# Turning attention probabilities with VectorE's block transposes and SBUF-to-SBUF transfers in a two-layer transformer kernel

## The reference, cut to what matters

```python
def _L0_ffn_ref(x, q_w, k_w, v_w, o_w, sel_v_w, sel_o_w, route_scale):
    H, E, P, K = (8, 8, 128, 2)
    gate_v = _get_sel_gate(x, sel_v_w, rs)      # [b, s, h, e], two of eight experts not zero
    gate_o = _get_sel_gate(x, sel_o_w, rs)
    xv = jnp.einsum('bsd,hedp->bshep', x, v_w.reshape(H, E, D, P))
    v = jnp.einsum('bshep,bshe->bhsp', xv, gate_v)
    att = jax.nn.softmax(jnp.einsum('bhqp,bhkp->bhqk', q, k) * SCALE, axis=-1)
    ctx = jnp.einsum('bhqk,bhkp->bqhp', att, v)
    weighted = ctx[:, :, :, None, :] * gate_o[..., None]
    out = jnp.einsum('bshep,hepd->bsd', weighted, o_w.reshape(H, E, P, D))
```

## Time and profile before

| | us |
|---|---|
| median of 3 runs | 3138.77 |
| lowest, highest run | 3130.59, 3141.73 |
| span of the profiled execution | 3102.4 |
| PE busy in it | 2958.3 |
| DVE busy | 2183.4 |
| ACT busy | 1926.7 |
| POOL busy | 1838.9 |

### The profile page before, as it was taken

One profiled execution on the slowest core, in us unless ns is written; L12 is line 12 of the kernel. 1 busy time (PEld: TensorE's weight loads), 2 busy tenths in 40 slices (PEclk: granted clock), 3 DMA queues, 4 the chain that ended last, 5 costly groups with the idle time before them and its releaser, 6 DMA issues. The chain is left out here.

```text
span 3102.4 us, 53399 instructions
## 1 busy us (share of the span) xinstructions
PE 2958.3 (95%) x17672; PEld 2071.1 (67%) x17672; DVE 2183.4 (70%) x4152; ACT 1926.7 (62%) x4366; POOL 1838.9 (59%) x2333
## 2 busy tenths in 40 slices
PE   4999999999999999999999999999999987899998
PEld 2666666666666666666666666666667675567675
DVE  7777888877778888777788887777777655235243
ACT  1576666676667666666666666666666743353634
POOL 2466666676666666676766676666666645433330
PEclk7899999999999999999999999999999989899999
DMA  5000001100100011001000110011001011233222
GB/s 171 21 22 23 22 22 33 32 23 26 44 26 22 23 32 33 23 23 37 29 22 22 33 32 23 23 37 29 23 22 40 16 42 44 65 96 104 86 77 87
DMA packets 140048, 124.71 MB, mean 40 GB/s; under 512 B 28662, under 2 KB 122304, under 8 KB 139680
## 3 DMA queue, kind: packets, MB, share of 16 engines
q1 hardware_dynamic: 127312, 88.75, 10.2%
q0 software_dynamic: 10160, 30.17, 3.1%
q10 hardware_dynamic: 2304, 2.36, 0.4%
HBM read 97.47 MB, written 29.28 MB: 41 GB/s over the span
## 5 line engine op out<-in xcount | busy, mean ns | idle before, releaser
L1340 DVE TENSOR_REDUCE m_peaks<-m_ring 128x1 f32<-128x512 f32 x1024 | 636.7, 681 | 95.3 <-PE m_ring L299 95.1
L1072 ACT ACTIVATE m_expA<-m_ring 128x512 f32<-128x512 f32 x1024 | 536.3, 607 | 120.5 <-PE m_ring L372 102.3
L933 POOL TENSOR_TENSOR m_vprod<-m_vprod 128x512 f32<-128x512 f32 x256 | 334.3, 1306 | 451.5 <-DVE m_vprod L1353 327.1
L1043 ACT ACTIVATE m_prob<-m_ring,m_negs 128x512 f32<-128x512 f32 x512 | 350.8, 691 | 285.9 <-DVE m_negs L1388 285.4
L943 POOL TENSOR_TENSOR m_oprod<-m_oprod 128x512 f32<-128x512 f32 x256 | 329.4, 1287 | 258.9 <-ACT m_oprod L1012 255.2
L350 PE MATMUL m_ring<-m_probT,m_vs 128*128 128x256 f32 x2048 | 464.4, 380 | 5.8 <-DVE m_vprod L1353 5.2
L350 PEld LDWEIGHTS m_ring<-m_probT,m_vs 128*128 128x128 f32 x2048 | 386.3, 190 | 68.4 <-issue 13.3
L1378 DVE TENSOR_REDUCE m_negs<-m_ring 128x1 f32<-128x512 f32 x512 | 344.3, 684 | 115.3 <-PE m_ring L105 113.2
L1353 DVE TENSOR_TENSOR m_vprod<-m_ring,m_gate 128x512 f32<-128x512 f32 x512 | 342.2, 687 | 112.4 <-PE m_ring L105 99.5
L1053 ACT ACTIVATE m_probT<-m_ring 128x512 f32<-128x512 f32 x512 | 294.0, 610 | 63.2 <-PE m_ring L338 61.8
L1012 ACT ACTIVATE m_oprod<-m_ring,m_go 128x128 f32<-128x128 f32 x1024 | 292.0, 372 | 34.6 <-PE m_ring L105 23.7
(11 more groups left out here) (322 smaller groups left out, 5558.3 us busy)
## 6 DMA issues: line engine op xcount, KB each, us to landing
m_wraw<-in_v_w SPq DMA_DIRECT2D x32, 512.0 KB, 4.1
m_qf<-q_dram SPq DMA_DIRECT2D x128, 128.0 KB, 2.7
m_wraw<-in_o_w SPq DMA_DIRECT2D x32, 512.0 KB, 4.3
q_dram<-m_kf SPq DMA_DIRECT2D x24, 256.0 KB, 4.4
listed<-in_pad SPq DMA_DIRECT2D x6, 897.0 KB, 11.5
m_xg<-listed SPq DMA_DIRECT2D x39, 138.0 KB
m_rows<-answers SPq DMA_DIRECT2D x8, 512.0 KB, 4.1
sums_dram<-m_sumsT ACTq DMA_DIRECT2D x128, 18.0 KB
```

The source lines that it names most:

```text
L933: vchain(pool.tensor_tensor(vprod[:, 0:512], vprod[:, 0:512], vprod[:, 512:1024], ALU.add))
L1043: act.activation(prob[t % 2][:, c * 512:(c + 1) * 512], ring.home["scores", n, t, c][:, :], ACT.Exp, bias=neg[t % 2], accum_out=den[n % 2] ...
L1072: act.activation(expA[hh][:, c * 512:(c + 1) * 512], ring.home["scT", n, k, hh, c][:, :], ACT.Exp)\
L1340: v.tensor_reduce(peaks[:, t, hh, c:c + 1], ring.home["peaks", n, t, hh, c][:, :], AX.X, ALU.max)\
```

## The change

- `turn` and `keep_turned` are gone. DVE turns a whole tile of probabilities with one instruction, `turn_probs` (128x1024). It transposes each block of 32x32 on its own and writes to a single tile `turned`, which holds a group of two query tiles.
- SP carries the blocks to their places in `move_probs`: 16 transfers a group, one for each pair of 32-row blocks (a, b), each 32 partitions by 8 pieces of 64 elements (256 B). `probT` is one tile instead of two. A move waits for both transposes of its group and for the `weigh` before it; `weigh` waits for the move; `turn_probs` of an even tile waits for the move of the group before.
- The queries of a group now lie in `probT` in blocks of 32 that alternate between the two tiles. `keep_ctx` and `lower_ctx` put them back through their access patterns.
- `gate_outputs` on DVE is left for tiles 1, 3, 5 and 7. For even tiles ACT scales both halves.
- The order on every engine is new, and so is the place of the loads on SP. `load_layer1` comes one head earlier.

The new functions, from the diff:

```diff
+                def turn_probs(n, t):
+                    if n not in steps:
+                        return
+                    k = TPB * n + t
+                    v.wait_ge(probs_made, 2 * k + 2)
+                    if t % 2 == 0 and k:
+                        v.wait_ge(probs_moved[(k // 2 - 1) % 2], moved(0, k // 2 - 1))
+                    v.transpose(turned[:, :, t % 2, :], prob[t % 2][:, :].rearrange("p (c r) -> p c r", r=32))\
+                        .then_inc(probs_turned, 1)
...
+                def move_probs(n, g):
+                    if n not in steps:
+                        return
+                    sp.wait_ge(probs_turned, 8 * n + 2 * g + 2)
+                    if 4 * n + g >= 1:
+                        sp.wait_ge(ctx_made, 4 * n + g)
+                    by_key = turned[:, :, :, :].rearrange("p (k b) t j -> p b k (t j)", b=4)
+                    for a in range(4):
+                        for b in range(4):
+                            sp.dma_start(probT[32 * b:32 * b + 32, :, 64 * a:64 * a + 64],
+                                         by_key[32 * a:32 * a + 32, b, :, :]).then_inc(probs_moved[g % 2], 16)
...
-                    pe.wait_ge(probT_kept, 16 * n + 4 * g + 4)
+                    pe.wait_ge(probs_moved[g % 2], moved(n, g))
...
-                def scale_outputs(n, t):
+                def scale_outputs(n, t, c):
...
-                for i in steps:
-                    load_queries(i + 1)
-                    load_outputs(i)
-                    if i + 2 in steps:
-                        load_values(i + 2)
+                for i in range(-5, N0 + 5):
+                    load_values(i + 1)
+                    move_probs(i - 1, 3)
+                    load_queries(i + 1)
+                    move_probs(i, 0)
+                    if i == N0:
+                        load_early_heads()
+                    if i == N0:
+                        load_early_rden()
+                    batch_loads(i)
+                    move_probs(i, 1)
+                    load_outputs(i)
+                    move_probs(i, 2)
```

More of the change, by code:

```diff
@@ L225, in layer0 @@
         den = [m.sbuf(f"den{k}", [P, TPB, 2]) for k in range(2)]
-        probT = [m.sbuf(f"probT{k}", [P, TPB, 2 * P]) for k in range(2)]
+        probT, turned = m.sbuf("probT", [P, TPB, 2 * P]), m.sbuf("turned", [P, T // 32, 2, 32])
         ctxT = [m.sbuf(f"ctxT{k}", [PS, 2, 2 * P]) for k in range(2)]
@@ L1773, in _ @@
+                    find_largest(i + 2, 3, 0)
+                    gate_values(i + 3, 2, 0)
+                    find_largest(i + 2, 3, 1)
+                    gate_values(i + 3, 2, 1)
+                    join_largest(i + 2, 3)
                     take_peaks(i + 3, 0, 0, 0)
```

576 lines of the change are left out of this document (275 added, 301 removed).

## The result

| | before | after |
|---|---|---|
| median, us | 3139.38 | 3523.11 |
| lowest, highest run | 3130.59, 3141.73 | 3513.58, 3532.33 |
| span of the profiled execution | 3102.4 | 3530.5 |

The changed kernel takes 1.123 times as long (95% interval 1.120 to 1.126), 384 us more, where I forecast 27 us less. The time is outside the range.

A forecast was written before the change was run, and what follows sets the result against it. PE was taken to bound the layer-0 loop at 75.9 us a head. From the span of 3102.4, 34 us off and 10 on gave 3078, with 36.4 carried over 3115, stated as 3112 us; range 3015 to 3190.

The forecast's parts named there:

- ends: Last group's uncovered move and the early heads' loads queued behind it on SP: 10 us added, 5 to 20.
- step 2: PE's new order breaks fours of 32-row products: 27 sets a head, before 16; 0.43 us each, 4.7 us a head lost.
- The 36.4 us: Excess of the runs' median over the profiled span before, added to 3078 us to give 3115 us.
- Step 1: PE's identity products go in each head of the layer-0 loop: 6.9 us a head, all on the path.
- Step 3: DVE gets eight transposes a head at 1.2 us, going from 59.8 to 66.6 us: 1.1 us a head of stall.
- step 4: SP's 16 transfers a group take about 8.5 us, hidden behind longer PE work between weighs: no cost to PE.
- rival A: Broken sets cost little, falling in PE's gaps; DVE and PE meet at about 71.5 us a head: 3013 us, chance 0.22.
- rival C: DVE is the bound: transposes take 2.1 us and more, a head takes 77 us: 3182 us, chance 0.1.
- rival B: SP's moves come late between second and fourth weigh; at 12.5 us a move 3 us a head: 3205 us, chance 0.18.
- my upper bound of 12.5: Length in us of a move on SP at the worst row's 40 ns a packet: 10.3 us, 12.5 with the landing.
- The signs: Right: head intervals 74 to 75.5 us, 16 issues 6 to 6.5; wrong: weigh or even transpose waiting a microsecond each.

The follow-up runs named there:

- wide_pieces: The changed kernel with the same 16 transfers a move, in 128 pieces of 512 B instead of 256 of 256 B: 3511.47 us, ratio 1.118.
- half_rows: The changed kernel with 16 partitions in each transfer of a move in place of 32: 3491.07 us, ratio 1.112.
- before_broken: The kernel before with its sets of four 32-row products broken in 11 places, 25 sets a head instead of 16: 3270.25 us, ratio 1.040.
- before_quarter_turns: The kernel before with one identity product in each turn in place of four, ACT's copies kept: 3088.71 us, ratio 0.984.
- no_moves: The changed kernel with one transfer in each move instead of 16, all waits kept: 3323.37 us, ratio 1.055.
- from_dram: The changed kernel with moves that read a weight tensor in DRAM in place of turned, in the same 16 transfers: 3344.04 us, ratio 1.065.
- no_moves_no_turns: The changed kernel with one transfer a move and, after the first group, transposes of 128x32 in place of 128x1024: 3205.16 us, ratio 1.019.

## Why the prediction was wrong

The moves through this kernel's order, by the time from the first issue to the landing: 2.1 us 3323, 8.0 us 3329, 9.4 us 3344, 11.7 us (wide_pieces) 3511, 11.8 us (half_rows) 3491, 12.0 us 3523. That and the other pairs give each step its number.

| term | forecast, us | measured, us |
|---|---|---|
| identity products off PE | -214 | -65 (49 for three quarters) |
| eleven broken sets | +146 | +151 (124 for nine; but 16 came) |
| transposes on DVE, stall | +34 | +113 |
| moves | 0 | +213 |
| ends | +10 | about +11 |
| sum | -24 | +423, the whole is +386 |

The measured terms come from different kernels and so need not add up; they do within 10%, which is partly luck: the first and the second are scaled up from smaller edits, and by the trace of the changed kernel the second is larger (step 2). The ends are an estimate: what is left when 2.3 further heads at 11.2 us are taken from the 37 us outside the 31 intervals. The 36.4 us that I carried over from span to runs don't lie around the span, since the changed kernel's own time is only 2 us above its span (3532.33 and 3530.5). The profiled execution of before was quick behind the loop: 718.9 us from its last marker on, where before_broken took 763.9, before_quarter_turns 758.7 and the changed kernel 796.1.

Steps 1, 3 and 4 failed and step 2 fell short. The largest miss is in step 4, the issue of a move. But moves without cost would not have brought the time into my range of 3015 to 3190: no_moves takes 3323 us, by the others.

**Step 1, identity products: wrong in size.** I took PE's time as time, since PE was busy 75.4 of 75.9 us. before_quarter_turns shows that a PE that is freed meets its readers at once: 49 of 160 us came back as time, 30%. Its waits in the trace are for ACT and DVE, 10 us in eight heads. That the gate is their nearness through the seven PSUM tiles, which a busy share of 95% hides, is my reading; no run gave PE more tiles. And the 65 us leave out what ACT's copies were worth, so they may be too few.

**Step 2, broken sets: the price right, the number short.** 0.43 us each, and rival A falls. Late claims break further sets at run time: starts within 0.06 us of each other taken as one set, a head holds 33, not 27, and held 17 before, not 16. So 16 sets more came, not 11. By the distances of their starts the 64 products hold PE 14.0 us a head in place of 7.6, and 6.4 x 31 = 197 us, where I had 146; waits inside a set and some time at 1.2 GHz are in it. The sign, products busy over 13 us a head, came as 21.2.

**Step 3, transposes: the duration right, the stall wrong.** 1.23 us for 1.2, DVE's 64.7 us near 66.6, rival C's condition (2.1 us) not met. But my price of 0.2 us for a microsecond of DVE work, read from light and heavy heads at 56 and 63 us of DVE, is 0.3 to 0.6 at 58 to 65 us with a PE that has less work. And I let the split of gate_outputs count for nothing; alone it costs 82 us, though in the new order hardly any.

**Step 4, moves: the mechanism right, one term wrong, and it is the largest miss, 213 us for nothing.** The term that failed is the issue, 0.40 us from the loads of o_in in the earlier trace rows. In the moves it is 0.65 from start to start, so that a move takes 12.0 us and not 8.5. Of the 0.25 us the source in SBUF is 0.16 (0.65 for 0.49 in from_dram); the rest came with the shape. The two distances that the move had to fit were right: the even transpose, which I had 9 us or more behind the weigh's end, is ready 8.9 us behind the move's start, and the 10.8 us between the third and the fourth weigh came as 10.2. At 8.0 us the move is hidden, as I had it. The loss starts at 9 us, where the transpose is ready, and not at the 11 us of rival B, which took PE's distance. The 12.0 us are near my upper bound of 12.5, reached for another reason than I gave (the packets took 25 ns, not 40), so that rival B's length was luck. It then gave 3205 in all, from 1.5 us in each of two gaps and as much for DVE. What came is one gap a head: the move is late, the even transpose by 3.1 us, then softmax, then the PSUM tile that weigh claims, and PE waits 4.1 us where no_moves waits 1.0; then weigh runs at 1.2 GHz, 2.1 us longer. These two are 5.2 us a head, some 160 of the 213 us. From 9.4 to 12.0 us the time rises by 179 us, 69 for each.

**What no step had: the clock.** Before, it was 1.00 in the loop. In the changed one 12 us a head pass at 1.2 GHz. An estimate from the distances of PE's starts: products that began at 1.2 GHz held PE 5.7 us a head longer than the same pairs of products did at 2.4 GHz; it is 4.5 in no_moves and 1.1 in no_moves_no_turns. So about half of the 11.2 us a head that the change lost in its loop are the clock. This is within the measured terms, and is why the moves are dearer than their waits in the trace. The wait of 4.1 us is followed by 1.2 GHz in 30 of 31 heads; but not each wait counts, for at the same place from_dram waits 0.6 us a head more than no_moves and has the higher clock in its eight heads, 0.96 for 0.94. What lets the clock fall at the other places, as at 1340, stays open.

The signs: transposes and DVE's time right; intervals of 86.3 in place of 74 to 75.5, issues of 10.4 us in place of 6 to 6.5, weigh and the even transpose waiting, as under "wrong" for rival B, by three to four microseconds in one group and not by one in each.

## What to carry to other kernels

Price a transfer's issue from a row with the same source, destination and shape, and if there is none take the whole spread of the rows, here 0.32 to 0.60 us. Where the length of a chain decides whether it is hidden, take the shortest of the distances that it must fit, here the 8.9 us to the transpose and not the 10.2 us to weigh, and give the loss beyond it the larger chance if the bounds straddle it. Work taken off an engine that is 95% busy is only worth its time if the next engine and the buffers between them have room: leave the work out of the kernel as it is and measure before building the rest. In a loop balanced to a few per cent a new wait can cost more than itself: here one of 4.1 us a head was followed by work at half the clock in 30 of 31 heads, one of 1.6 us in 3.

## What the runs showed of the chip

- A transfer from SBUF to SBUF that SP issues took 0.60 to 0.61 us of issue, for 128 and 256 pieces, 16 and 32 partitions, 256 and 512 B; 0.45 us for the same shape from DRAM. Landing was 2.1 us in both. With other shapes the source doesn't decide: the store of 64 KB from m_dens took 0.35 us, the load of m_dens 0.58, the loads of o_in 0.32.
- The issue of a transfer from DRAM that follows such moves grew with them: that of o_w from a median of 0.42 us before to 0.60 after. It was 0.60 behind a single transfer (no_moves) too, and 0.45 behind moves from DRAM. Why, the runs don't tell.
- A 32x32-block transpose on DVE in fp32, SBUF to SBUF: 0.20 us for 32 columns, 0.70 for 512, 1.23 for 1024.
- Packets between SBUF tiles took 25 ns with 256 B and 39 ns with 512 B, with 16 transfers in a row; with 256 B from DRAM 18 ns (from_dram).
- Nine further sets of 32-row products a head left the clock at 1.00. In the new order, with waits besides, it was 0.90 to 0.98.
